# Attention weights ATT made by VectorE with one multiply-add per sequence instead of two GpSimd passes, and a shorter way to the key sums

## The reference

```
Q  = elu(x Wq + bq) + 1;   Kf = elu(x Wk + bk) + 1;   V = x Wv + bv
KV = sum over tokens (Kf * V);   sumK = sum over tokens (Kf)
att = Q * KV / (Q * sumK + 1e-6)
y = gelu(att Wo + bo);          x = layer_norm(y + x)
h = gelu(gelu(x W1 + b1) W2 + b2);   x = layer_norm(h + x)
```

## Time and profile before

| | |
|---|---|
| median of 3 runs | 3431.5 us (3430.92 to 3431.95) |
| span of the profiled execution | 3428.6 us |
| its own time beside the span | not given apart; the median lies 2.9 us above the span |
| DVE busy in the span | 2711.6 us, 79% |
| PE busy in the span | 3029.2 us, 88% |
| POOL busy | 1323.7 us, of which L285 and L289 are 305.9 and 316.7 us |
| ACT busy | 1927.6 us, 56% |
| granted TensorE clock, mean | 0.945 |

### The profile page before, as it was taken

The page is one execution under the profiler, slowest core; times in us unless marked ns, Lnnn a source line. Parts: engine busy times, 40 slices in busy tenths (PEclk is TensorE's granted clock), DMA queues, the critical chain, the costliest instruction groups (busy, mean ns, idle before and its releaser), DMA issues. The chain is left out here.

```text
span 3428.6 us, 44182 instructions
## 1 busy us (share of the span) xinstructions
PE 3029.2 (88%) x11560; PEld 2029.0 (59%) x11561; DVE 2711.6 (79%) x8902; ACT 1927.6 (56%) x2995; POOL 1323.7 (39%) x1039
## 2 busy tenths in 40 slices
PE   5698989898989898999899989998999976998995
PEld 4465656565656565666566655665566644776553
DVE  8879888988898889888988898889888834763111
ACT  4566666666666666666666666666666622442221
POOL 5325343534353435343534353435443323333002
PEclk9899999999999999999999999999999987997998
DMA  4001100100011001000100010001000001003312
GB/s 102 17 1 24 25 16 18 24 25 16 18 24 25 16 18 24 25 16 18 24 25 16 18 24 25 16 18 24 18 24 4 1 0 49 0 0 131 100 40 74
DMA packets 212286, 93.22 MB, mean 27 GB/s; under 512 B 146792, under 2 KB 207984, under 8 KB 212048
## 3 DMA queue, kind: packets, MB, share of 16 engines
q1 hardware_dynamic: 209408, 83.30, 9.6%
q0 software_dynamic: 2640, 7.21, 0.6%
HBM read 80.24 MB, written 10.22 MB: 26 GB/s over the span
## 5 line engine op out<-in xcount | busy, mean ns | idle before, releaser
L350 PE MATMUL PS<-XTHI,WHI 128*128 128x512 f32 x1536 | 672.6, 438 | 38.1 <-DVE EK L654 27.9
L285 POOL TENSOR_TENSOR INV<-INV,CE 128x512 f32<-128x512 f32 x256 | 305.9, 1195 | 984.1 <-DVE INV L697 984.1
L646 DVE SCALAR_TENSOR_TENSOR RK<-RK,EK 128x128 f32<-128x128 f32 x1024 | 599.6, 638 | 28.7 <-ACT RK L515 0.5
L351 PE MATMUL PS<-XTLO,WHI 128*128 128x512 f32 x1536 | 610.7, 398 | 0.0
L352 PE MATMUL PS<-XTHI,WLO 128*128 128x512 f32 x1536 | 609.9, 397 | 0.0
L398 PE MATMUL Y<-ATT,WO 128*128 128x512 f32 x1024 | 468.5, 612 | 59.8 <-POOL ATT L289 59.4
L398 PE MATMUL Y<-H,W2S 128*128 128x512 f32 x1024 | 465.9, 609 | 51.9 <-DVE R L708 50.4
L289 POOL TENSOR_TENSOR ATT<-INV,CC 128x512 f32<-128x512 f32 x256 | 316.7, 1237 | 195.5 <-PE Y L398 177.9
L398 PEld LDWEIGHTS Y<-ATT,WO 128*128 128x128 f32 x1024 | 197.7, 196 | 301.0 <-issue 298.2
L350 PEld LDWEIGHTS PS<-XTHI,WHI 128*128 128x128 f32 x1536 | 291.4, 190 | 133.2 <-issue 42.3
L398 PEld LDWEIGHTS Y<-H,W2S 128*128 128x128 f32 x1024 | 197.0, 195 | 290.4 <-issue 227.2
(11 more groups left out here) (195 smaller groups left out, 5440.7 us busy)
## 6 DMA issues: line engine op xcount, KB each, us to landing
STAGE<-L_attn_Wk SPq DMA_DIRECT2D x128, 64.0 KB, 2.1
STAGE<-L_attn_Wv SPq DMA_DIRECT2D x128, 64.0 KB, 2.1
STAGE<-L_attn_Wq SPq DMA_DIRECT2D x128, 64.0 KB, 2.1
WO<-L_attn_Wo SPq DMA_DIRECT2D x8, 1024.0 KB, 5.5
W2S<-L_attn_W SPq DMA_DIRECT2D x8, 1024.0 KB, 6.1
STAGE<-L_attn_W SPq DMA_DIRECT2D x64, 128.0 KB, 3.7
RAW<-L_ffn_r_gate SPq DMA_DIRECT2D x8, 512.0 KB, 3.5
RAW<-L_ffn_r_up SPq DMA_DIRECT2D x8, 512.0 KB, 3.6
```

The source lines that it names most:

```text
L285: nc.gpsimd.tensor_tensor(r3, r3, spread(CE[:, e, :], SEQ), ALU.mult).then_inc(att_s, 1)
L350: nc.tensor.matmul(out, whi[:, kc, :], xhi[:, kc, :], start=(kc == 0), stop=False)
L351: nc.tensor.matmul(out, whi[:, kc, :], xlo[:, kc, :], start=False, stop=False)
L646: ins = nc.vector.scalar_tensor_tensor(RK[:, p, seq(b)], RK[:, p, seq(b)], 0.0, EK[:, p, seq(b)], ALU.add, ALU.add, accum_out=SUMK[:, p, b ...
```

## The change

The two POOL passes go away; DVE gets `weigh`, four TENSOR_SCALAR per chunk, one for each sequence, with CE and CC as operands that hold one number per partition. It stands in DVE's order at fixed places: chunks 0 to 2 together after `queries` of chunk 3, then one chunk behind each `queries` of chunks 4, 5 and 6, and chunks 6 and 7 each right behind their `inverses` at the slot's end, ahead of XTLO. ACT's chunk makes exp(k+b) straight from PSUM, so one ACT pass over 128x512 per chunk is gone and EK is made ahead of RK. DVE's key sum becomes min(RK + 1, EK) in the same instruction, which is the same function. ES comes from one reciprocal of sumK * 1e6, RSK is gone, and there are four small statistics where there were five.

```diff
-            def attend(l, t, c):
-                pool.wait_ge(recip, n + 1)
-                pool.wait_ge(stat, n * 5 + 5)
-                nc.gpsimd.tensor_tensor(r3, r3, spread(CE[:, e, :], SEQ), ALU.mult).then_inc(att_s, 1)
...
-                nc.gpsimd.tensor_tensor(ATT[:, c, :].rearrange("p (b s) -> p b s", b=TS), r3,
-                                        spread(CC[:, e, :], SEQ), ALU.add).then_inc(att, 1)
...
-                nc.scalar.activation(EK[:, p, :], PS[:, half, :], ACT.Relu, scale=-1.0,
-                                     bias=BNEG[:, 0, c:c + 1]).then_inc(nk, 1)
+                nc.scalar.activation(EK[:, p, :], PS[:, half, :], ACT.Exp, bias=BA[:, 0, c:c + 1]).then_inc(ek, 1)
                 nc.scalar.activation(RK[:, p, :], PS[:, half, :], ACT.Relu, bias=BA[:, 0, c:c + 1]).then_inc(rk, 1)
-                act.wait_ge(nk, n + 1)
-                nc.scalar.activation(EK[:, p, :], EK[:, p, :], ACT.Exp, scale=-1.0).then_inc(ek, 1)
...
-                    ins = nc.vector.scalar_tensor_tensor(RK[:, p, seq(b)], RK[:, p, seq(b)], 0.0, EK[:, p, seq(b)],
-                                                         ALU.add, ALU.add, accum_out=SUMK[:, p, b:b + 1])
+                    ins = nc.vector.scalar_tensor_tensor(RK[:, p, seq(b)], RK[:, p, seq(b)], 1.0, EK[:, p, seq(b)],
+                                                         ALU.add, ALU.min, accum_out=SUMK[:, p, b:b + 1])
...
-                nc.vector.reciprocal(RSK[:, p, :], SUMK[:, p, :]).then_inc(stat, 1)
-                dve.wait_ge(stat, n * 5 + 2)
-                nc.vector.tensor_scalar(ES[:, p, :], RSK[:, p, :], EPS_ATT, None, ALU.mult).then_inc(stat, 1)
+                nc.vector.reciprocal(ES[:, p, :], SUMK[:, p, :]).then_inc(stat, 1)
...
+            def weigh(l, t, c):
+                g, e = l * TILES + t, c % IRING
+                n = g * HC + c
+                dve.wait_ge(recip, n + 1)
+                dve.wait_ge(stat, n * 4 + 4)
+                if c == 0 and not (type(g) is int and g == 0):
+                    dve.wait_ge(y_mm, g)
+                for b in range(TS):
+                    ins = nc.vector.tensor_scalar(ATT[:, c, seq(b)], INV[:, e, seq(b)], CE[:, e, b:b + 1],
+                                                  CC[:, e, b:b + 1], ALU.mult, ALU.add)
+                ins.then_inc(att, 1)
```

More of the change, by code:

```diff
@@ L97, in attention_stack @@
         KVS = sb("KVS", [P, 2, TS])
-        RSK = sb("RSK", [P, 2, TS])
         CC = sb("CC", [P, IRING, TS])
@@ L127, in attention_stack @@
             sem(n) for n in ("k_mm", "v_mm", "q_mm", "y_mm", "yt_mm", "x1t_mm", "h_mm", "z_mm", "zt_mm", "xt_mm"))
-        b_neg, nk, ek, rk, nq, eq, rq, y_act, x1_hi, h_act, z_act, xt_hi, log, inv = (
-            sem(n) for n in ("b_neg", "nk", "ek", "rk", "nq", "eq", "rq", "y_act", "x1_hi", "h_act", "z_act", "xt_hi",
+        b_neg, ek, rk, nq, eq, rq, y_act, x1_hi, h_act, z_act, xt_hi, log, inv = (
+            sem(n) for n in ("b_neg", "ek", "rk", "nq", "eq", "rq", "y_act", "x1_hi", "h_act", "z_act", "xt_hi",
                              "log", "inv"))
@@ L136, in attention_stack @@
             sem(n) for n in ("res1", "mv1", "x0", "n1", "x1", "res2", "mv2", "n2", "mv0"))
-        half_set, att_s, att, w_hi, w_lo, r1, r2, xn_s, xn, r0 = (
-            sem(n) for n in ("half_set", "att_s", "att", "w_hi", "w_lo", "r1", "r2", "xn_s", "xn", "r0"))
+        half_set, att, w_hi, w_lo, r1, r2, xn_s, xn, r0 = (
+            sem(n) for n in ("half_set", "att", "w_hi", "w_lo", "r1", "r2", "xn_s", "xn", "r0"))
         def piece_incs(k):
@@ L294, in slot @@
                 tile = exists(l, t)
-                nl, nt = slot_of(l, t + 1)
-                more = exists(l, t + 1)
                 splits = load and t == TILES - 2
@@ L307, in slot @@
                         rstd(RSTD[:, 1, :], MV[:, 1, :, 1], EPS1, mv2, 2 * g, r2, g)
-                    if more:
-                        attend(nl, nt, c - 1)
                     if splits_w1 and 2 <= c < 2 + PIECES - HC:
@@ L321, in slot @@
                                                 ALU.add).then_inc(xn, 1)
-                if more:
-                    attend(nl, nt, HC - 1)
             nc.gpsimd.memset(SPARE[:, :], 0.0).then_inc(xn, 1)
@@ L332, in _ @@
                 split_piece(0, k, True)
-            for c in range(HC):
-                attend(0, 0, c)
             for k in range(HC, PIECES):
@@ L657, in keys @@
                 ins.then_inc(kv_sum, 1)
[L658 to L662 removed]
+                nc.vector.tensor_scalar(SUMK[:, p, :], SUMK[:, p, :], TINY, 1.0 / EPS_ATT, ALU.max,
+                                        ALU.mult).then_inc(stat, 1)
+                dve.wait_ge(stat, n * 4 + 1)
+                nc.vector.reciprocal(ES[:, p, :], SUMK[:, p, :]).then_inc(stat, 1)
                 dve.wait_ge(kv_sum, n + 1)
+                dve.wait_ge(stat, n * 4 + 2)
                 if not (type(n) is int and n < IRING):
                     dve.wait_ge(att, n - (IRING - 1))
[L666 to L667 removed]
+                nc.vector.scalar_tensor_tensor(CC[:, e, :], KVS[:, p, :], 1.0 / EPS_ATT, ES[:, p, :], ALU.mult,
+                                               ALU.mult).then_inc(stat, 1)
+                dve.wait_ge(stat, n * 4 + 3)
                 nc.vector.tensor_tensor(CE[:, e, :], CC[:, e, :], ES[:, p, :], ALU.mult).then_inc(stat, 1)
@@ L680, in queries @@
                 dve.wait_ge(q_exp, n + 1)
-                dve.wait_ge(stat, n * 5 + 3)
+                dve.wait_ge(stat, n * 4 + 2)
                 for b in range(TS):
@@ L743, in slot @@
                         inverses((LAST - 1) * HC + c, c)
+                        weigh(LAYERS - 1, TILES - 1, c)
                 if tile:
@@ L751, in slot @@
                     queries(nl, nt, 3)
+                    for c in range(3):
+                        weigh(nl, nt, c)
                     keys(nl, nt, 4)
@@ L756, in slot @@
                     queries(nl, nt, 4)
+                    weigh(nl, nt, 3)
                 if tile:
@@ L767, in slot @@
                     queries(nl, nt, 5)
+                    weigh(nl, nt, 4)
                 if not first:
@@ L781, in slot @@
                     queries(nl, nt, 6)
+                    weigh(nl, nt, 5)
                 if not first:
@@ L791, in slot @@
                     inverses(n - 2, HC - 2)
+                    weigh(nl, nt, HC - 2)
                     residues(n - 1, HC - 1)
                     inverses(n - 1, HC - 1)
+                    weigh(nl, nt, HC - 1)
                 if exists(l, t + 3):
@@ L833, in _ @@
             queries(0, 0, 1)
+            weigh(0, 0, 0)
             input_lo(1, 1)
@@ L837, in _ @@
                 queries(0, 0, c)
+                weigh(0, 0, c - 1)
             input_lo(2, 2)
@@ L840, in _ @@
             queries(0, 1, 0)
+            weigh(0, 0, HC - 1)
             slot(0, 0, first=True)
```

6 lines of the change are left out of this document (removed).

## The result

| | before | after |
|---|---|---|
| median | 3431.2 us (3430.39 to 3431.95, 4 runs) | 3450.05 us (3448.10 to 3450.99, 4 runs) |
| ratio, 95% interval | | 1.0061 (1.0046 to 1.0076) |
| span of the profiled execution | 3428.6 us | 3449.3 us |
| DVE busy | 2711.6 us | 2714.7 us |
| POOL busy | 1323.7 us | 706.2 us |

GpSimd has lost half its work and ScalarE 121 us; VectorE is as busy as before, and the kernel is 19 us slower where I had forecast 7 us less. (The quotient of the two medians is 1.0055, inside the interval.)

The account below looks back on a forecast made before the run. Layer nearly PE-bound (315.1 of 344.8 us), its time hanging on VectorE's lateness with R, X1LO and XTLO. -0.85 us a layer gives -6.6, first tile +1, last tile -1.5: -7 us, 3424 us; range 3378 to 3474.

Parts of the forecast that it names:

- step 5: Weight pieces no longer wait behind `attend` and fall on VectorE's SBUF work: +1.7 us in the long stretch, +1.1 in slot 0.
- Step 1: `attend` leaves GpSimd, so VectorE stands still less: -14.0 us in the long stretch, 3.7 less in slot 0.
- Steps 2 and 3: One small statistic fewer per chunk, -1.3 us, and EK ready earlier at key chunk 3, -1.0, both in the long stretch.
- long stretch: VectorE from its wake-up in slot 1 to X1LO of slot 2, 126.7 us without real gap; forecast sum -0.2 us.
- Step 4: `weigh` comes to VectorE at 0.257 us each, four make 1.03: +14.4 us for 13 chunks in the long stretch.
- Slots 3, 0 and 1: The layer's other slots: slot 3 -0.9 us, slot 0 +0.45, slot 1 -0.2, by shifted XTLO, X1LO and ATT waits.
- Slower, by the pieces: Pieces without `attend` between them hold VectorE's grown SBUF work at full price: 8.7 us more a layer, 3491, half 3458; chance 0.2.
- Dear weigh: `weigh` on VectorE costs 0.325 us each, 4.9 us more a layer: 3462 us; chance 0.1.
- cheap weigh: `weigh` on VectorE costs 0.190 us each, 4.8 us less a layer: 3387 us; chance 0.15.
- PE's slow stretches go: PE's half-speed matmuls behind its long waits vanish as waits shrink, some 3 + 3 us a layer: 3378 us; chance 0.1.

Follow-up runs that it names:

- hold_two: The changed kernel with one wait more: GpSimd starts weight piece 0 of slot 2 only when XTLO is made; 0.9967 of the kernel before.
- keys_only: The kernel before with only the keys' part of the change (ScalarE's key passes, key sum, four statistics), `attend` staying on GpSimd; 0.9877 of the kernel before.
- hold_acthi: hold_two with the high parts of the weight pieces after the first layer made by ScalarE, low parts on GpSimd; 0.9733 of the kernel before.
- quarter_weigh: The changed kernel with `weigh` making only one of a tile's four sequences after the first tile; 0.9597 of the kernel before.
- thin_pieces: The changed kernel with only 16 columns of each weight piece split from the second layer on; 0.9560 of the kernel before.
- hold_recip: The changed kernel with GpSimd waiting for each chunk's refined reciprocal where `attend` stood, without `attend`'s work; 1.0007 of the kernel before.
- act_weigh: hold_two with ATT made by ScalarE, four activations for each chunk, and no `weigh` on VectorE; 1.0176 of the kernel before.
- keys_thin: keys_only with only 16 columns of each weight piece split after the first layer; 0.9477 of the kernel before.

## Why the prediction was wrong

The point forecast was 3424, 0.2% faster, and the kernel was 0.6% slower; 3450 lies in the range given.

*The step that failed* is step 5, "The pieces move": "They no longer wait behind `attend`, so in slot 2 piece 4 runs straight behind the standard deviation ...; so do pieces 9 to 11 in slot 0". I followed those and not pieces 0 and 1, which had waited behind `attend` of chunk 7. The amount was about right: standing still under pieces rose from 174 to 191 us, 2.4 for each of seven layers, and I had 2.8. Its place was not: 5.3 us of it now lie ahead of XTLO, where PE has nothing else to do, and PE's wait there went from 1.28 to 6.09 us. My rows did not even hold that wait of slot 2. I had bounded the amount on both sides and given no price to the place. hold_two shows it: with piece 0 behind XTLO a layer is 4.5 us shorter than in the changed kernel and the kernel at 0.9967.

*Step 1*, `attend` gone: held. The key sum's mean falls from 733 to 459 ns in the stretch from key chunk 3 to X1LO (I said near 500), and VectorE's standing still in the whole program from 554 to 315 us, by walking both traces (each VectorE instruction above the undisturbed time of its form, laid beside the GpSimd row that it overlaps).

*Steps 2 and 3*, the keys: right in sign and under-sized. 1.3 and 1.0 in the long stretch, and little elsewhere, against 5.4 us a layer by the ratio (5.6 by the profiles): 2.6 by the statistic and 2.9 by ScalarE's pass. Of the 5.6, 3.4 are waits and 1.8 the clock, for which my sum had no term. I took them as gains of one stretch; all four slots gain. That 0.10 us would fall away with one statistic, and that the other three keep their forms, was wrong too: CC takes another form and now waits for ES.

*Step 4*, the price of `weigh`: 0.257 us each, forecast and measured, with 0.33 to 0.34 for one. By the page "VectorE: DVE Perf Modes" of the Trainium skill, section "The TRN2 errata — SBUF-src ops pay a fixed extra latency per instruction", it would be an estimate of 0.127; the trace disagrees here too, and the same section says itself that its row under-predicts single instructions. What `weigh` costs against `attend` was under-sized: +14.4 against -14.0 in the long stretch and near nothing in the others, but +4.3 a layer from keys_only to hold_two, 1.8 of them in the first two windows and 2.5 in the other two. By the table 1.8 of the 4.3 are waits and 1.7 the clock. VectorE's time for it is 1024 times 0.257, 263 us, and 18.6 us idle before it. What `attend` held of VectorE in keys_only is 240 to 265 us in the walk, by what is taken as the undisturbed time of each form, so VectorE is occupied for some 17 to 42 us more with `weigh`, against 31 that hold_two loses to keys_only. The size fits; no run shows where it falls, and why the difference vanishes in hold_acthi stays open.

So the forecast's near balance rested on two errors of opposite sign: the keys too small (5.4 to 5.6 us a layer against 2.3 and little more) and `weigh` against `attend` too cheap (4.3 against near nothing). Its share on the path was counted rightly (56%, and 58% in PE's waits); the clock that goes with the waits was left out. That hold_two at 0.9967 lies near the 0.998 of the forecast is therefore luck and no support for its sum.

*Slots 3, 0 and 1*: sum -0.65 forecast. Windows three and four together are 0.3 us shorter than before in the layer shown, and 0.5 us longer on average over the seven. The wait in slot 0 did move, from X1LO (4.76 us) to the x1 transposes, as I had not said.

*The rivals.* Of the two on the slower side "Slower, by the pieces" (0.2) had the right agent; its mechanism was more standing still, and what happened was the same standing still in a worse place. "Dear weigh" fell with 0.257, "cheap weigh" too. "PE's slow stretches go" did not happen here (0.94 in both first windows); in keys_only it did in part: time at half clock falls from 23.9 to 17.6 us a layer, a third of its gain.

*What the profile should show*: `weigh` 0.26 apart, yes; L646's heir near 500 ns, yes, 459; the pieces' standing still in the long stretch inside 13 to 20 us, yes, some 16; ATT waits under 1, no, 6.09 at slot 2's start, for XTLO; R and X1LO together still 10 us, no, 0.4 and 0.1; layer within 3 us of 344.8, no, by a little, 3.1.

## What to carry to other kernels

When work leaves an engine's queue, list everything that stood behind it there and where each item's own dependence lets it start now, with the first item of the queue's next stage included; it is mainly the place of a blocking pass and not its length that changed here. Price a saving on an engine that is busy nine tenths of a layer in every stage, and give the clock a term of its own: quarter_weigh and thin_pieces brought back 83% and all of what VectorE was relieved of, 58% and 71% of it as PE's waits and most of the rest as clock. And time the parts of a compound change apart: here a 1.2% gain was hidden in a loss.

## What the runs showed of the hardware

- `weigh`, a TENSOR_SCALAR with one input in SBUF and two operands with one number per partition, stands still under GpSimd's passes as the key sum does: 4.05 and 5.06 us for four instead of 1.12. XTLO, which reads PSUM and SBUF, keeps 1.21 us beside a piece (1657.45 in hold_recip, where a low part runs from 1657.53) and without. The rule in the Trainium skill, page "SBUF — State Buffer", section "Who interferes with whom", puts the first down to a two-port mode; the rows agree that it contends.
- That standing still came back in the span at its own size: 24 us a layer less under pieces, 25 us a layer gained, 17.2 of them as PE's waits and 6.5 as clock.
- The granted clock adds to a gain in waits, in no fixed ratio: before to keys_only, 3.4 us of idle time and 6.3 us less at 1.2 GHz a layer, 1.8 us counted once; before to hold_acthi, 11.4 us of idle time and 7.8 us less at 1.2 GHz; in act_weigh 34.6 us at 1.2 GHz with 30.7 of idle time, where the changed kernel has 26.3 with the same 30.7. In keys_thin, with 12.9 us of idle time a layer, no whole layer has a stretch at 1.2 GHz left.
- The same work, four times 128 columns with two per-partition operands, starts 0.385 us apart on ScalarE and 0.257 on VectorE.
